# Two group sums of a half in one PSUM bank, behind one signal

## The reference, cut

```python
def _round(x, w, b, gamma, beta, src, dst, etype):
    h = jax.nn.relu(_bn(x, gamma, beta))
    h = jnp.einsum('nd,od->no', h, w) + b
    h3 = h.reshape(N, T, D)
    msg = h3[src, etype]
    return jax.ops.segment_sum(msg, dst, num_segments=N)

h_new = _round(features, w1, b1, g1, be1, src, dst, etype)
h_new = _round(h_new, w2, b2, g2, be2, src, dst, etype)
# h_new + features, layer norm, then:
h = x @ W_in
W_ij = (ssp(f_ij @ Wf1 + bf1) @ Wf2 + bf2) * f_ij_cutoff
out = jax.ops.segment_sum(h[idx_j] * W_ij, idx_i, num_segments=x.shape[0])
# ssp(out @ Wo1 + bo1) @ Wo2 + bo2, residual, layer norm
```

## Time and profile before

| What | us |
| --- | --- |
| Timed executions, median of 3 | 8408.23 |
| Lowest and highest of them | 8375.33, 8417.95 |
| The profiled execution | 8335.65 |
| Its span | 8333.8 |
| Busy: PE, PEld | 4465.5, 3450.3 |
| Busy: DVE, ACT | 3576.1, 1301.6 |
| Busy: POOL | 4693.9 |

### The profile page before, as it was taken

How to read it: one execution, slowest core, us unless ns; L and a number is a source line. 1 busy time by engine, 2 the same in 40 slices (tenths; PEclk the granted TensorE clock), 3 DMA queues, 4 the chain that set the end, 5 groups by cost and what they waited for, 6 DMA issues and landing times.

```text
span 8333.8 us, 89560 instructions
## 1 busy us (share of the span) xinstructions
PE 4465.5 (54%) x21555; PEld 3450.3 (41%) x21555; DVE 3576.1 (43%) x7435; ACT 1301.6 (16%) x3301; POOL 4693.9 (56%) x4809
## 2 busy tenths in 40 slices
PE   5233232323345444444545556666677676676787
PEld 3222222222233333333333334555555565565676
DVE  6222222222244444444445554333333455555577
ACT  2000000000011000000000004444444333333303
POOL 3666666666644666666665555665665544444413
PEclk8555556556667777777777877666666778878799
DMA  6111111111133111111112222222222344444476
GB/s 230 46 44 44 46 44 45 44 45 45 45 103 117 43 42 43 42 43 44 43 43 64 71 70 82 82 82 83 82 82 83 109 137 136 136 138 135 140 245 212
DMA packets 406720, 710.67 MB, mean 85 GB/s; under 512 B 103887, under 2 KB 180850, under 8 KB 405940
## 3 DMA queue, kind: packets, MB, share of 16 engines
q1 hardware_dynamic: 255766, 387.96, 14.9%
q0 software_dynamic: 150912, 322.24, 13.5%
HBM read 509.88 MB, written 199.90 MB: 85 GB/s over the span
## 4 chain that ended last, share of the span: by engine, by line
another core or an unknown queue 35%; PE 26%; issue 18%; DVE 15%; DVEq 3%; ACT 2%; POOL 1%; SPq 1%; DMA 0%; ACTq 0%; POOLq 0%
PE banks L1467 6%; PE banks L1363 6%; PE banks L1456 3%; DVE work L818 3%; PE banks L1512 3%; PE banks L1340 2%; PE banks L1324 2%; DVE biased L1187 2%; DVE first_place L830 1%; PE banks L1481 1%; DVE work L828 1%; DVE work L1083 1%; DVE work L833 1%; PE banks L1339 1%
## 5 line engine op out<-in xcount | busy, mean ns | idle before, releaser
L506 POOL DMA_INDIRECT edge_rows<-messages,idx_stage x1568 | 1498.1, 955 | 1060.0 <-issue 574.3
L550 POOL DMA_INDIRECT sorted_rows<-edge_rows,idx_stage x784 | 799.5, 1020 | 717.4 <-DVE edge_rows L1191 497.9
L550 POOL DMA_INDIRECT sorted_rows<-buf_a,idx_stage x784 | 793.4, 1012 | 652.5 <-DVE buf_a L1191 417.3
L506 POOL DMA_INDIRECT buf_a<-messages,idx_stage x784 | 748.4, 955 | 464.2 <-issue 234.1
L506 POOL DMA_INDIRECT buf_x<-messages,idx_stage x784 | 748.1, 954 | 412.0 <-issue 238.0
L1467 PE MATMUL banks<-work,buf_a 128*128 128x128 f32 x4744 | 723.6, 310 | 456.2 <-DVE buf_x L1149 294.8
L1363 PE MATMUL banks<-onehot,edge_rows 128*128 128x128 f32 x3136 | 572.6, 345 | 724.3 <-DVE buf_a L904 369.1
L1363 PEld LDWEIGHTS banks<-onehot,edge_rows 128*128 128x128 f32 x3136 | 545.9, 256 | 849.7 <-issue 446.9
L1467 PEld LDWEIGHTS banks<-work,buf_a 128*128 128x128 f32 x4744 | 663.5, 221 | 550.0 <-DVE buf_x L1149 326.5
L1339 PE MATMUL banks<-work,ones_b 128*128 128x392 bf16 x392 | 166.4, 424 | 1197.7 <-DVE first_place L830 640.8
L1363 PE MATMUL banks<-onehot,buf_x 128*128 128x128 f32 x1568 | 321.2, 378 | 879.6 <-DVE buf_a L904 566.2
(11 more groups left out here) (165 smaller groups left out, 6562.2 us busy)
## 6 DMA issues: line engine op xcount, KB each, us to landing
buf_a<-sorted_rows SPq DMA_DIRECT2D x593, 288.0 KB
messages<-work SPq DMA_DIRECT2D x196, 320.0 KB, 2.2
buf_a<-dst_rows SPq DMA_DIRECT2D x198, 256.0 KB
buf_a<-in_attr SPq DMA_DIRECT2D x198, 128.0 KB
buf_a<-h_in SPq DMA_DIRECT2D x396, 64.0 KB
edge_rows<-messages,idx_stage POOLq DMA_INDIRECT x1568
buf_x<-messages,idx_stage POOLq DMA_INDIRECT x784
buf_a<-messages,idx_stage POOLq DMA_INDIRECT x784
```

Source lines behind the costliest of these rows:

```text
L506: nc.gpsimd.indirect_dma_start(gathered[p][h][:, t, :], None, source, bass.IndirectOffsetOnAxis(ap=idx_stage[:, h, t:t + 1], axis=0),).the ...
L550: nc.gpsimd.indirect_dma_start(sorted_rows, bass.IndirectOffsetOnAxis(ap=idx_stage[:, 2 * u + h, t:t + 1], axis=0), msg_halves[2 * u + h][ ...
```

## The change

The two sums of half h now lie side by side in bank 4 + h: `ps_sums[h][j]` is columns j x 128 to (j + 1) x 128. TensorE signals once, behind the second sum of a half, and VectorE's two adds wait for that same value. TensorE waits for adds only before the first sum of a half, and for the two adds of the half before the last, which had the same bank; `s_acc` starts at SUMS2 = 4 for this. In round 1 the count matmuls stand between the two sums, ahead of the second, so that the half's signal comes after them; `s_count` and VectorE's wait for it are gone. The number of matmuls and their operands are the same.

```diff
-        ps_agg = [ps_b[j][:, 0:WINDOW] for j in range(2)]
+        ps_sums = [[ps_b[h][:, j * WINDOW:(j + 1) * WINDOW] for j in range(2)] for h in range(2)]
...
+        SUMS2 = 4
...
             def accumulate(p, acc, r, h, j, bases):
                 g = r * 4 + (2 * h + j)
-                dve.wait_ge(s_agg[p], g + 1)
-
-                dve.wait_ge(s_acc[p], g + SLOT2)
+                dve.wait_ge(s_agg[p], r * 2 + (h + 1))
+
+                dve.wait_ge(s_acc[p], g + SUMS2)
                 at = acc[:, ds(bases[2 * h + j], WINDOW)]
-                nc.vector.tensor_tensor(at, at, ps_agg[j], ALU.add).then_inc(s_acc[p], 1)
+                nc.vector.tensor_tensor(at, at, ps_sums[h][j], ALU.add).then_inc(s_acc[p], 1)
...
                 build_onehot(p, r + h, 1 - h)
-                if p == 0:
-                    dve.wait_ge(s_count, k + SLOT2)
                 build_high(p, r + h, 1 - h)
...
             for p in range(2):
-                pe.sem_inc(s_acc[p], SLOT2)
+                pe.sem_inc(s_acc[p], SUMS2)
...
             def count_blocks(k, h, i):
                 pe.wait_ge(s_hot[0], k + 1)
                 for j in range(2):
-                    last = nc.tensor.matmul(ps_counts[i], ones_b[:, :], high_hot[:, h, j, :], start=False, stop=False)
-                last.then_inc(s_count, 1)
+                    nc.tensor.matmul(ps_counts[i], ones_b[:, :], high_hot[:, h, j, :], start=False, stop=False)
...
-                    pe.wait_ge(s_acc[p], g + 1)
+                    if j == 0:
+                        pe.wait_ge(s_acc[p], g + 2)
+                    elif p == 0:
+                        count_blocks(r * 2 + h, h, i)
                     for t in range(GROUP_TILES):
-                        last = nc.tensor.matmul(ps_agg[j], rows_in_slot[:, j * GROUP_TILES + t, :], onehot[:, h, j * GROUP_TILES + t, :],
+                        last = nc.tensor.matmul(ps_sums[h][j], rows_in_slot[:, j * GROUP_TILES + t, :], onehot[:, h, j * GROUP_TILES + t, :],
                                                 start=(t == 0), stop=(t == GROUP_TILES - 1))
-                    last.then_inc(s_agg[p], 1)
-                if p == 0:
-                    count_blocks(r * 2 + h, h, i)
+                last.then_inc(s_agg[p], 1)
```

More of the change, by code:

```diff
@@ L275, in gnn_program @@
         s_hot = [sem(f"high_onehot_{i}") for i in range(2)]
-        s_count, s_ranked, s_picked, s_passed, s_placed, s_placed_out = (sem(n) for n in (
-            "blocks_counted", "edges_ranked", "ranks_picked", "places_passed", "places_staged", "places_kept"))
+        s_ranked, s_picked, s_passed, s_placed, s_placed_out = (sem(n) for n in (
+            "edges_ranked", "ranks_picked", "places_passed", "places_staged", "places_kept"))
         s_closed, s_reached, s_steps, s_table = (sem(n) for n in (
@@ L997, in count_beyond @@
                 round_loop(0, buf_a, 0, ITERS, 0, True)
-                dve.wait_ge(s_acc[0], GROUPS + SLOT2)
+                dve.wait_ge(s_acc[0], GROUPS + SUMS2)
                 with dve.Fori(0, CHUNKS_IN) as c:
@@ L1007, in count_round @@
                         bases = load_bases(r)
-                        dve.wait_ge(s_acc[0], r * 4 + SLOT2)
+                        dve.wait_ge(s_acc[0], r * 4 + SUMS2)
                         node_stats(1, buf_a, r - CHUNK_ITERS)
@@ L1015, in rank_beyond @@
                 round_loop(1, buf_x, FIRST_ITERS, ITERS, 1, True)
-                dve.wait_ge(s_acc[1], GROUPS + SLOT2)
+                dve.wait_ge(s_acc[1], GROUPS + SUMS2)
                 y_chunk(0)
@@ L1028, in chunk_step @@
                     scale_rows(m - 1)
-                dve.wait_ge(s_acc[1], r * 4 + SLOT2)
+                dve.wait_ge(s_acc[1], r * 4 + SUMS2)
                 y_chunk(m)
@@ L1311, in _ @@
             for s in (s_yc, s_sd, s_rsd, s_rows, s_x1, s_hrow, s_soft, s_fsoft, s_msg, s_hcopy,
-                      s_fz, s_fo, s_fy, s_added, s_count, s_passed, s_placed, s_placed_out):
+                      s_fz, s_fo, s_fy, s_added, s_passed, s_placed, s_placed_out):
                 pe.sem_inc(s, SLOT2)
```

## The result

The changed kernel takes 8493.0 us (median of 4 runs, 8475.5 to 8498.4) against 8413.1 us (median of 4, 8375.3 to 8425.5): a ratio of 1.010, 95% interval 1.007 to 1.013, so 60 to 112 us slower. The forecast had the sign and the place right, and a size more than double what came: +174 us.

A forecast was written before the change was run, and what follows sets the result against it. No engine was full; GpSimd's gathers waited 781 us for indices staged behind late TensorE signals. 0 + 21 + 0 + 153 + 0 = +174 us on the 8408 us median gave 8582 us, range 8480 to 8760 (8 in 10: 8210 to 8810).

The forecast's parts named there:

- (1): Both rounds, TensorE's signals: removing signals of sums and counts gives 0, with -781 us as the other bound.
- rival B: Both rounds: signals themselves are slow, some 5 to 8 us each, so fewer give up to -781 us, 7627 us; chance 0.10.
- slow stretch: While gathers run, TensorE's signals come very late, apparently in proportion to matmuls, such as starts 1.41 us apart in round 2.
- (2): Round 1, VectorE: two adds behind one signal delay staging by 0.41 us in each of 52 pauses, +21 us.
- (3): Round 1, TensorE: it may run a half ahead, counted as 0 for GpSimd's pauses.
- rival A: Round 1: TensorE running ahead removes GpSimd's pauses, -314 us there, -161 us overall, 8247 us; chance 0.22.
- (4): Round 2, VectorE: the first add waits for both sums, lengthening each of 102 pauses from 4.57 to 6.07 us, +153 us.
- (5): Round 2, TensorE: next rank matmuls wait behind both sums, about 1.3 us per half, at most 255 us; taken as 0.
- Rival C: Whole kernel: nothing measurable, as some 20 to 30 vanished round 1 pauses cancel round 2's loss, 8408 us; chance 0.13.
- Rival D: Round 2: the lost TensorE overlap shows fully, +255 us on top of +174, 8837 us; chance 0.07.

The follow-up runs named there:

- spare signals: Kernel before with two of eight gathers per half, plus an unawaited signal at each sum's first three matmuls: 5687.8 us where the full kernel before takes 8329 us.
- two-gather kernels: Kernel before and changed kernel, each with six of the eight gathers of a half left out: 4751.6 and 5064.7 us where the full kernel before takes about 6660 us.
- one wait changed: Kernel before with two of eight gathers per half, round 2's first add also waiting for the second sum's signal: 6009.1 us.

## Why the prediction was right, and where its size was off

(1) *One signal for two sums, 0.* Right. The case itself is the test of rival B, with eight gathers and the slow stretch: 392 signals are gone from round 1, of sums and of counts, and it takes 2291.0 us in place of 2289.9. The spare signals say the same from the other side (1176 more in a round, 0.4 us), with two gathers for each half, where the signals are delayed less.

(2) *Round 1, +0.41 us for each pause.* The step grew as it was forecast, from 0.20 to 0.62 us, but the +0.39 of the mean wait is in the main luck. Among the pauses with both adds outstanding the mean went up by 0.03 us (6.65 to 6.68) and the median by 0.29 (6.64 to 6.93); the mean over all waits rose because the 13 shorter pauses with one add outstanding (4.93 us) became none. With three pauses fewer, all of them together grew by 4 us, and round 1 by 1.1 us in place of +21. It was the smaller term.

(3) *Lookahead in round 1, 0, with rival A at -314 us.* The pauses did not vanish (48 of 51 over 3 us are left). In the two-gather kernels the change moves round 1 by +2.4 us on a free chip. On the slow chip the changed kernel's round 1 is 12 us shorter than before's (658.2 against 670.5, one execution each), so there may be something in rival A, but little.

(4) *Round 2, 102 x (6.07 - 4.57) = +153 us.* The mechanism was right, and this is **the term that was mis-sized**: the pauses of round 2 grew by 88 us, and the round by 102.9. The step that failed compared a mean over all waits with one sampled pause and multiplied by all 102. Only 65 pauses were of the first kind. They grew by 1.60 us each, as the two steps had said (1.62), which is +104 us; the 26 that were of the second kind already gained nothing (6.26 to 6.13 us), and two pauses are gone. The prediction had named this as the way to come out below its range, "if part of the pauses were of the second kind already", but had not counted them, though the trace of the kernel before holds the count.

(5) *Lost overlap on TensorE, bound 255 us, taken as 0.* Right for the case: the add that is waited for starts 3.15 us behind the last gather, where it started at 3.10, so the pauses are not longer by it, and what it can have cost there is at most the 17 us of short idle times. Bare, with two gathers for each half, the chain costs 292 us on a free chip and 325 on the slow one, more than the bound. The bound had the waiting nearly right, 1.3 us for each half against 0.99 and 1.10 measured, and left out that TensorE's mean clock falls where it idles longer (0.94 to 0.88, and 0.93 to 0.87), which is up to another 99 and 110 us. Under eight gathers all of this is covered on a free chip: a half takes 8.57 us of chain and 10.1 us of GpSimd.

Rival C asked for round 1 to pay for round 2, which it didn't. Rival D, +255 on top, would have needed TensorE's two halves to take longer than GpSimd's 20 us. The last assumption, that the slow stretch belongs to the kernel, was never written down as one. It doesn't come with the kernel: on the free chip on which the whole change ran it costs 0.1% (0.02 to 0.21%), and its halves and variants on two others cost 0 to 0.1%. That the measured time fell into the range rests on the kernel having run where the slow stretch is.

## What to carry to other kernels

Joining two signals into one saves nothing by itself, and the wait for the joint one starts at the later event: look at what is queued behind the first wait on its engine, and at who waits for that. Here it was a rank step that the other engine needs for its next half. Work that another engine waits for belongs ahead of the joint wait: with the rank steps there, 227 of 325 us came back. Then ask what covers the chain: 1.5 us for each half cost nothing as long as GpSimd needed 10.1 us and the chain 8.6. When a pause is to be sized, count its kinds in the trace, and don't set the mean of all waits against one sample. And look at TensorE's clock when a wait is added to its chain: as much as a third of the price here was slower matmuls.

## What the hardware showed that I had not expected

Chips differ, or the states that they are in. The same program takes 6654 to 6668 us on three chips and 8329 to 8413 us on two occasions elsewhere, 25% more, and nearly all of it lies in stages in which GpSimd issues indirect transfers: the rounds take 2290 and 2433 us in place of 1970 to 1977 each, and the convolution 2899 to 2947 in place of 2028 to 2038, while the output after it takes 375 to 380 us on all of them. A gather is 0.95 us long on each. With two gathers for each half the slow chip is slower in round 1 by 670.5 / 623.3, 8%, and in round 2 not at all, which fits a slow stretch that needs dense gathers.

The trace's record of semaphore increments hints at where it is. A round's gathers send 1568 x 16 = 25088 increments. On the free chips 25078 to 25088 of them are on record, in the trace of the kernel before 4454 in round 1 and 5774 in round 2 (two gathers for each half: 6209 and 6272 of 6272 for the kernel before on the free chip, 3109 and 5501 with the one wait changed on the slow one). That increments of the transfers hold up TensorE's signals would fit this and the 29 us between a sum and its add, but no run here tests it, and it stays a guess.

TensorE's granted clock in round 1 is 0.59 in the case, where its work comes in pauses and bursts, and 0.50, the lower of its two levels (1.2 GHz), on the free chips, where its work trickles without a pause; eight matmuls of a sum take 1.92 us there and 1.05 us at the full clock. On the free chips it costs nothing, since GpSimd sets the round. In round 2 there, the change lowers the clock as well, from 0.80 (change in round 1 alone) to 0.77 (whole change), and TensorE's matmuls go from 1226 to 1296 us, all of it under GpSimd's gathers.
